# A gather, pair-product and attention-pooling tower in fp32: the last tile's bands stored by three queues and loaded by two, their wrapped columns added by TensorE, and layer 1 of rows 0 to 255 issued ahead of the tail's pooling

## What is computed

```python
row, col = np.triu_indices(33, k=1)
inner = e[:, row] * e[:, col]                        # 512 x 528 x 128
fm = relu(einsum('bpd,ad->bpa', inner, attn_W) + attn_b)
attn = softmax(einsum('ba,bpa->bp', gnn, fm), axis=1)
pooled = einsum('bp,bpd->bd', attn, inner) * 100.0
h = concatenate([gnn, pooled, gnn], axis=1)
h = maximum(h @ W_top1 + b_top1, 0)                  # 384 -> 512
h = maximum(h @ W_top2 + b_top2, 0)                  # 512 -> 256
y = h @ W_top3                                       # 256 -> 1
```

## Time and profile before

| | |
|---|---|
| Median of 3 runs | 651.45 us (651.18 to 651.52) |
| The profiled execution | 656.16 us |
| Its span, first to last instruction | 654.4 us |
| Granted TensorE clock, mean | 0.999 of full |
| TensorE matmul busy | 641.9 us (98%) |
| TensorE weight loads busy | 328.1 us (50%) |
| VectorE, ScalarE, GpSimd busy | 403.6, 417.4, 268.8 us (62%, 64%, 41%) |
| Largest group: L466, TensorE | 480.8 us |
| Its consumer: L700, ScalarE | 406.0 us |
| L531, TensorE, the pooling of `band` | 33.5 us |

### The profile page before, as it was taken

The page is one execution under the profiler, slowest core; times in us unless marked ns, Lnnn a source line. Parts: engine busy times, 40 slices in busy tenths (PEclk is TensorE's granted clock), DMA queues, the critical chain, the costliest instruction groups (busy, mean ns, idle before and its releaser), DMA issues.

```text
span 654.4 us, 22667 instructions
## 1 busy us (share of the span) xinstructions
PE 641.9 (98%) x9596; PEld 328.1 (50%) x9596; DVE 403.6 (62%) x426; ACT 417.4 (64%) x797; POOL 268.8 (41%) x208
## 2 busy tenths in 40 slices
PE   6998999999999999999999999999999999999998
PEld 2444444444444555544444555544444555544566
DVE  3564655656664677676655577766655567764763
ACT  2665666666777566676777556667677666677651
POOL 6787876685656422244746522244101011100010
PEclk9999999999999999999999999999999999999999
DMA  3211111011091111000092111000026011030010
GB/s 117 83 37 37 30 36 30 25 30 64 18 31 27 28 32 26 16 13 18 14 32 30 24 32 30 16 18 6 1 14 15 7 17 18 7 21 8 16 25 8
DMA packets 51286, 17.29 MB, mean 26 GB/s; under 512 B 47553, under 2 KB 48321, under 8 KB 51202
## 3 DMA queue, kind: packets, MB, share of 16 engines
q1 hardware_dynamic: 44738, 6.03, 11.3%
q0 software_dynamic: 4288, 8.66, 5.5%
q10 hardware_dynamic: 2176, 1.32, 0.7%
HBM read 14.10 MB, written 1.89 MB: 24 GB/s over the span
## 4 chain that ended last, share of the span: by engine, by line
PE 91%; DVE 2%; POOL 2%; DMA 2%; another core or an unknown queue 1%; issue 1%; ACT 0%; DVEq 0%; ACTq 0%
PE x_ps L466 66%; PE s_ps L478 16%; PE m_ps L531 4%; POOL rows L364 2%; DVE inner L757 2%; PE m_ps L523 1%; DMA rows<-in_table,idx 1%; PE s_ps L571 1%; PE x_ps L571 1%; PE x_ps L531 1%; DMA idx_in<-in_ids 0%; PE x_ps L560 0%; DVE e_t L809 0%; PE m_ps L560 0%
## 5 line engine op out<-in xcount | busy, mean ns | idle before, releaser
L700 ACT ACTIVATE fm<-x_ps,ab 128x352 f32<-128x352 f32 x768 | 406.0, 555 | 204.3 <-PE x_ps L466 184.2
L466 PE MATMUL x_ps<-inner,attn_w_t 128*32 128x352 f32 x6144 | 480.8, 459 | 2.2 <-issue 0.9
L466 PEld LDWEIGHTS x_ps<-inner,attn_w_t 128*32 128x32 f32 x6144 | 201.5, 110 | 229.7 <-issue 149.4
L757 DVE TENSOR_TENSOR inner<-e_t 128x2112 f32<-128x2112 f32 (+1 forms) x128 | 302.0, 2359 | 19.3 <-PE x_ps L466 16.6
L364 POOL DMA_INDIRECT rows<-in_table,idx x128 | 213.0, 1664 | 196.5 <-PE s_ps L478 179.9
L478 PE MATMUL s_ps<-fm,gnn_col 128*32 128x256 f32 (+1 forms) x2048 | 138.0, 386 | 0.0
L773 DVE COPY gnn_col<-gnn_z 128x8 f32<-128x8 f32 (+1 forms) x120 | 23.9, 199 | 180.0 <-PE s_ps L478 173.0
L478 PEld LDWEIGHTS s_ps<-fm,gnn_col 128*32 128x32 f32 x2048 | 68.7, 110 | 62.4 <-issue 20.5
L392 POOL TENSOR_TENSOR band<-band 128x192 f32<-128x192 f32 (+1 forms) x39 | 26.3, 676 | 145.6 <-DMA band<-band_scratch 145.1
L531 PE MATMUL m_ps<-band,rows 128*32 128x132 f32 x912 | 33.5, 275 | 0.0
L531 PEld LDWEIGHTS m_ps<-band,rows 128*32 128x32 f32 x912 | 27.9, 109 | 7.1
(11 more groups left out here) (57 smaller groups left out, 86.5 us busy)
## 6 DMA issues: line engine op xcount, KB each, us to landing
band<-band_scratch SPq DMA_DIRECT2D x144, 18.4 KB
rows<-in_table,idx POOLq DMA_INDIRECT x128, 2.5
band_scratch<-zeros SPq DMA_DIRECT2D x1, 784.0 KB, 3.3
w<-in_W_top ACTq DMA_DIRECT2D x3, 256.0 KB
band_scratch<-attn SPq DMA_DIRECT2D x12, 64.0 KB
gnn_z<-in_gnn_pairs SPq DMA_DIRECT2D x1, 512.0 KB
w<-in_W_top ACTq DMA_DIRECT2D x1, 512.0 KB
gnn_t<-in_gnn_cols SPq DMA_DIRECT2D x1, 256.0 KB, 3.8
```

Of the source, the lines that this page charges most:

```text
L466: mm = pe.matmul(strip(x_ps[:, (ROUNDS * slot + r) % 4, 0:ROUND], c), strip_of(attn_w_t, c), round_of(inner, slot, r), start=True, stop=True)
L700: act.activation(round_of(fm, slot, r), x_ps[:, (ROUNDS * slot + r) % 4, 0:ROUND], ACT.Relu, bias=ab[:, 0:1]).then_inc(fm_ready, 1)
L757: dve.tensor_tensor(inner[:, slot, :, :].rearrange("p q (i k) -> p q i k", k=HOPS), flat(e, at, [[P * WIDE, P], [WIDE, QUADS], [1, FIELDS] ...
```

## The change

Four things are changed together. (1) The third stage's eight stores are spread: the SP queue issues two main and one turned, the ScalarE queue two main and one turned, the GpSimd queue two turned as before. The four loads behind them go two each to the SP and the GpSimd queue. (2) GpSimd's two folds of `tail_band` are gone. TensorE adds the wrapped columns itself: `tail_group` runs the four strips with 132 columns, then the same four strips again with the wrapped columns, 4 rows of 16, accumulated on the first 16 fields of each row. (3) Layer 1 of `T01` is issued right behind layer 1 of `T2`, before any tail group; the parts are reordered to `T2, T01, T3A, T3B` on all engines, and the tail's order is written anew. (4) Layer 1 of `T3A` uses another PSUM bank (`x_ps` bank 1 in place of 3), and waits are adapted.

```diff
--- before.py
+++ after.py
@@ -80,8 +80,8 @@
 TAIL_BEFORE = 2
 MLP_CUT = LAST * P + TAIL_ROW + TAIL_BEFORE * ROWS
 
-MLP_PARTS = ((LAST * P - P, LAST * P, 0), (LAST * P, MLP_CUT, 0), (0, 2 * P, P), (MLP_CUT, BATCH, MLP_CUT - LAST * P))
-T2, T3A, T01, T3B = range(len(MLP_PARTS))
+MLP_PARTS = ((LAST * P - P, LAST * P, 0), (0, 2 * P, P), (LAST * P, MLP_CUT, 0), (MLP_CUT, BATCH, MLP_CUT - LAST * P))
+T2, T01, T3A, T3B = range(len(MLP_PARTS))
 LAG = 2
 
 
...
@@ -249,7 +250,7 @@
             n = MLP_PARTS[part][1] - MLP_PARTS[part][0]
             if part == T01:
                 return chunk(m_ps[:, c // 2, :], c % 2, 2 * P, n)
-            return chunk(x_ps[:, 3, :] if part in (T2, T3A) else m_ps[:, 1, :], c, P, n)
+            return chunk({T2: x_ps[:, 3, :], T3A: x_ps[:, 1, :], T3B: m_ps[:, 1, :]}[part], c, P, n)
 
         def layer2_psum(part, c):
             n = MLP_PARTS[part][1] - MLP_PARTS[part][0]
@@ -279,19 +280,19 @@
                                 attn[32 * q + m0:32 * q + m1, SIDE * HOPS:PAIRS],
                                 allow_slow_non_contiguous=True).then_inc(done, 16)
 
-        def issue_tail_bands(queue, stage):
-
-            if stage == 1:
-                queue.wait_ge(band_stored, bands_per_stage * (LAST + 2))
-            else:
-                queue.wait_ge(band_stored, bands_per_stage * (LAST + 3) - 16 * 2)
-                queue.wait_ge(last_turned_stored, 16 * 2)
-            first, end = ((0, EARLY_GROUPS), (EARLY_GROUPS, TAIL_GROUPS))[stage - 1]
-            for r in range(GROUP):
-                queue.dma_start(tail_band[r * SIDE:(r + 1) * SIDE, first:end, r, :],
-                                flat(band_dram, (TAIL_ROW + GROUP * first + r) * BAND,
-                                     [[WIDE, SIDE], [GROUP * BAND, end - first], [1, WIDE]])
-                                ).then_inc(tail_band_loaded[stage - 1], 16)
+        def load_tail_band(queue, stage, r, done):
+
+            first, end = ((0, EARLY_GROUPS), (EARLY_GROUPS, TAIL_GROUPS))[stage]
+            queue.dma_start(tail_band[r * SIDE:(r + 1) * SIDE, first:end, r, :],
+                            flat(band_dram, (TAIL_ROW + GROUP * first + r) * BAND,
+                                 [[WIDE, SIDE], [GROUP * BAND, end - first], [1, WIDE]])
+                            ).then_inc(done, 16)
+
+        def wait_last_bands(queue):
+
+            queue.wait_ge(band_stored, bands_per_stage * (LAST + 2) + 16 * 3)
+            queue.wait_ge(last_stored_by_act, 16 * 3)
+            queue.wait_ge(last_stored_by_pool, 16 * 2)
 
 
         tail_banks = [x_ps[:, i, :] for i in range(4)] + [m_ps[:, 0, :]]
@@ -342,10 +343,14 @@
             for k in range(L_BATCHES):
                 load_band(k % 2, POOL_N * LAST + max(k - 1, 0), ROWS * k)
             issue_bands(sp, LAST + 1, STAGE_M[1], STAGE_M[2])
-            issue_tail_bands(sp, 1)
-
-            issue_bands(sp, LAST + 2, STAGE_M[2], STAGE_M[3], turned_around=(0, 1))
-            issue_tail_bands(sp, 2)
+            sp.wait_ge(band_stored, bands_per_stage * (LAST + 2))
+            for r in range(GROUP):
+                load_tail_band(sp, 0, r, tail_band_loaded[0])
+
+            issue_bands(sp, LAST + 2, STAGE_M[2], STAGE_M[3], main=(0, 1), turned_around=(0,))
+            wait_last_bands(sp)
+            for r in (0, 1):
+                load_tail_band(sp, 1, r, tail_band_loaded[1])
             sp.wait_ge(y_ready, len(MLP_PARTS))
             sp.dma_start(out.rearrange("b o -> o b"), y[:, :]).then_inc(y_stored, 16)
             sp.wait_ge(y_stored, 16)
@@ -442,13 +447,10 @@
                 fold_next(LAST - 1, k)
             for k in range(L_BATCHES):
                 fold_batch(k % 2, pool_per_tile[k % 2] * LAST + pool_per_batch * (k // 2 + 1))
-            for stage in range(2):
-                if stage == 1:
-                    issue_bands(pool, LAST + 2, STAGE_M[2], STAGE_M[3], main=(), turned_around=(2, 3),
-                                done=last_turned_stored)
-                pool.wait_ge(tail_band_loaded[stage], 16 * GROUP)
-                lo, hi = ((0, EARLY_GROUPS), (EARLY_GROUPS, TAIL_GROUPS))[stage]
-                fold(tail_band[:, lo:hi, :, :].rearrange("p g r w -> p (g r) w"), tail_band_folded)
+            issue_bands(pool, LAST + 2, STAGE_M[2], STAGE_M[3], main=(), turned_around=(2, 3), done=last_stored_by_pool)
+            wait_last_bands(pool)
+            for r in (2, 3):
+                load_tail_band(pool, 1, r, last_loaded_by_pool)
 
 
         @block.tensor
@@ -548,6 +550,21 @@
                 pool_batch(t, GPB * k, POOL_N * t + k + 1, k % 2, POOL_N * t + k - 1 if k >= 2 else None,
                            LEFT_GROUPS if k == POOLS else GPB)
 
+            def tail_group(g):
+
+                k = g // GPB
+                fields = rows[:, LAST % BUFFERS, GPB * L_BATCHES + g, :]
+                out = tail_banks[k][:, (g % GPB) * GROUP * FIELDS:(g % GPB + 1) * GROUP * FIELDS]
+                for c in range(STRIPS):
+                    sums = strip(out, c).rearrange("p (r w) -> p r w", w=FIELDS)
+                    pe.matmul(sums, strip_of(fields, c), tail_band[:, g, :, 0:FIELDS], start=True, stop=False)
+                for c in range(STRIPS):
+                    sums = strip(out, c).rearrange("p (r w) -> p r w", w=FIELDS)
+                    mm = pe.matmul(sums[:, :, 0:HOPS], strip_of(fields, c), tail_band[:, g, :, FIELDS:WIDE],
+                                   start=False, stop=True)
+                if g % GPB == GPB - 1 or g == TAIL_GROUPS - 1:
+                    mm.then_inc(pool_done, 1)
+
             def mlp_layer1(part):
 
                 pe.wait_ge(pool_summed, pools_through(part))
@@ -566,6 +583,8 @@
                 if part == T2:
                     pe.wait_ge(w23_loaded, 32)
                     pe.wait_ge(exp_done, LAST + 3)
+                if part == T01:
+                    pe.wait_ge(pool_read, POOL_N * LAST + L_BATCHES + 1)
                 for c in chunks:
                     for k in range(C1):
                         mm = pe.matmul(layer2_psum(part, c), w2[:, k, c * P:(c + 1) * P],
@@ -653,28 +672,26 @@
             scores(STEPS * TILES - 1, 1, stop=True, reopened=True)
             mlp_layer1(T2)
 
-            for g in range(TAIL_GROUPS):
-                k = g // GPB
-                if g == 0:
-                    pe.wait_ge(tail_band_folded, 1)
-                if g == TAIL_BEFORE * GPB:
+            mlp_layer1(T01)
+
+            pe.wait_ge(tail_band_loaded[0], 16 * GROUP)
+            for g in range(EARLY_GROUPS):
+                if g == GPB * 3:
                     mlp_layer2(T2)
-                if k == 3 and g % GPB == 0:
-                    mlp_layer3(T2)
-                    mlp_layer1(T3A)
-                    mlp_layer1(T01)
-                    mlp_layer2(T3A)
-                if g == EARLY_GROUPS:
-                    mlp_layer2(T01, (0,))
-                    pe.wait_ge(tail_band_folded, 2)
-                if k == TAIL_POOLS - 1:
-                    pe.wait_ge(pool_read, POOL_N * LAST + L_BATCHES - 1)
-                pool_group(tail_banks[k], g % GPB, rows[:, LAST % BUFFERS, GPB * L_BATCHES + g, :], tail_band[:, g, :, :],
-                           g % GPB == GPB - 1 or g == TAIL_GROUPS - 1)
+                tail_group(g)
+            mlp_layer2(T01, (0,))
+            mlp_layer1(T3A)
+            mlp_layer3(T2)
+            mlp_layer2(T01, (1,))
+
+            pe.wait_ge(tail_band_loaded[1], 16 * 2)
+            pe.wait_ge(last_loaded_by_pool, 16 * 2)
+            for g in range(EARLY_GROUPS, TAIL_GROUPS):
+                tail_group(g)
+            mlp_layer2(T3A)
+            mlp_layer3(T01)
+            mlp_layer1(T3B)
             mlp_layer3(T3A)
-            mlp_layer2(T01, (1,))
-            mlp_layer1(T3B)
-            mlp_layer3(T01)
             mlp_layer2(T3B)
             mlp_layer3(T3B)
 
@@ -741,6 +758,7 @@
                     relus(base + s, s % 2,
                           stage=LAST + STAGE_M.index(s - 1) - 1 if t == LAST and s - 1 in STAGE_M else None)
             exp_rows(LAST + 2)
+            issue_bands(act, LAST + 2, STAGE_M[2], STAGE_M[3], main=(2, 3), turned_around=(1,), done=last_stored_by_act)
             for part in range(len(MLP_PARTS)):
                 mlp_relu2(part)
                 mlp_out(part)
...
@@ -952,12 +970,12 @@
             row_max(LAST + 2, STEPS * TILES)
             mlp_relu1(T2)
             normalise(LAST + 2)
+            mlp_relu1(T01)
             for k in range(TAIL_POOLS):
                 row = TAIL_ROW + k * ROWS
                 pool_sum(LAST, POOL_N * LAST + L_BATCHES + k + 1, tail_banks[k], row, min(ROWS, P - row))
-                if k == TAIL_BEFORE - 1:
+                if k == TAIL_BEFORE:
                     mlp_relu1(T3A)
-                    mlp_relu1(T01)
             mlp_relu1(T3B)
```

(7 more changed lines are left out.)

## The result

The changed kernel takes 652.94 us (median of 9 runs, 652.44 to 653.92), the kernel before, measured with it, 651.45 (9 runs). The ratio is 1.0029, with a 95% interval of 1.0021 to 1.0038: 1.9 us slower, between 1.4 and 2.5. The medians are only 1.5 apart, since the changed kernel's runs lie in two clusters, five up to 652.94 and four from 653.60 to 653.92, and the median is the top of the lower one. Forecast were 653.2 us and slower by 1.76.

A forecast was written before the change was run, and what follows sets the result against it. TensorE's work was taken to bound the kernel, in an unbroken chain behind the last scores. Passes and order, 1.61 - 0.14 + 0.18 + 0.11 = +1.76 us on 651.45, gave 653.2 us, range 651.9 to 654.9.

The forecast's parts named there:

- What bounds the kernel: Tail behind the last scores: the chain runs through TensorE unbroken from 631.83 to 647.88, with no DMA or fold in it.
- The wrapped pass: Tail groups on TensorE: each added pass of 64 columns costs 0.115 us, 14 of them +1.61 us (1.48 to 3.19).
- The rival that priced a pass by what it issues: Tail groups: a wrapped pass costs 0.228 us, like one of 132 columns; +3.3 us, 654.8 us; chance 0.20.
- The order: TensorE's tail: one run of groups fewer -0.14, other work before the last four groups +0.18, end of tail +0.11 us.
- The gap that VectorE leaves there: Between layer 1 and layer 2 of `T3B`, ending at 3.58 and starting at 4.29 after the last group: 0.71 us.
- The sum: Whole tail: 1.61 - 0.14 + 0.18 + 0.11 = +1.76 us.
- The margin of the transfers: Ahead of group 10: late bands ready 1.3 us early before, loads landed some 4 us early after; faster transfers gain 0 us.
- The rival that ended faster: Ahead of group 10: before's timed runs wait for late bands, 3.2 us at 4.5 us lateness; 650.0 us; faster, chance 0.09.
- The unscaled sum: Whole kernel: the 4.7 us between profiled execution and median lies outside the tail, so +1.76 us is added unscaled.
- the second rival: Wait ahead of group 10: late bands were waited for in timed runs, which the change ends; 650.0 us; faster, chance 0.09.

The follow-up runs named there:

- 16-column kernel: The changed kernel with wrapped columns of only one row in four, so a pass's matmuls have 16 columns, not 64; 652.75 us, one run.
- the kernel with folds kept: The changed kernel with both folds back on GpSimd and no wrapped columns on TensorE; spread and new order stay; 651.42 us, ratio 1.0001 to before.
- the spread alone: The kernel before with only the third stage's stores on three queues and its loads on two; 650.90 us, ratio 0.9993 to before.

## Why the prediction was right

**What bounds the kernel.** Right, and shown from two sides: removing only the passes takes the time back to before, and making only the transfers faster leaves the tail at 20.95 us.

**The wrapped pass.** Forecast 0.115 us from the line through 132 and 352 columns, 14 of them 1.61. The chain shows 0.11 and 0.12, and the two pairs of kernels that differ by the passes show 1.64 and 1.55. The rival that priced a pass by what it issues, at 0.228, is refuted. The Trainium skill's floor of about 25 ns between the starts of two matmuls (page "TensorE: Matmul & The Clock Gate", section "Wait — 56ns, not 53.3ns?") would have made a pass 0.20 us, an estimate from that page, if it held for matmuls in different strips. The chain's 0.115 for eight records says it does not. I had written that before's trace neither confirms nor refutes the rule, from a mean of 28 ns a record. Read one by one, the same records already refute it between strips: in a group of before the matmuls of the four strips start at 633.219, 633.225, 633.232 and 633.239, and the next in the first strip 115 ns after its predecessor. The 16-column kernel, with 26 ns and more between starts in the same strip, doesn't contradict the rule within a strip.

**The order.** The term had the right sign and was too small, 0.15 in all; the traces show 0.35 to 0.45. Two errors are in it, and they partly cancel. Up to the end of the last group the forecast was 0.18 - 0.14 = +0.04; the kernel with folds kept has it at 640.39 - 626.75 = 13.64 us, before at 13.80, so it is -0.16. The missing gain is layer 1 of `T3A`, taken as unchanged: 1.06 us in before, 0.86 now. From the last group to the end of the last layer 2 the term was +0.11; it is 648.02 - 641.40 = 6.62 us, in the forecast 6.21, before 6.10, so +0.52. Layer 2 of `T3A` took 1.96, not 1.76, layer 1 of `T3B` 1.02, not 0.80, the last layer 2 1.99, not 1.92, and layer 3 of `T01` 0.95, not 1.02. The old values are steps between starts in before's chain, where a neighbour covers part of the operation: layer 1 of `T3B` is 0.80 as a step and 0.97 by its own row. A step's share in a chain isn't its price in another place. The gap that VectorE leaves there, 0.70 us, was forecast (0.71).

**The sum.** 1.76 forecast, 1.99 in the tail of the trace, 1.9 in the timed runs (1.4 to 2.5). The pass is the large term and was right for its reason. That the rest came within 0.2 us is in part luck, since the two errors of the order have opposite signs.

**The margin of the transfers.** Right in both orders, though smaller than forecast after the change: the late loads landed 639.89 - 636.60 = 3.3 us before TensorE took them, and some 4 were expected. The rival that ended faster, with bands awaited in the timed runs, finds no support: the spread alone shows at most 1.0 us of gain at the interval's end, and the tail doesn't move. That the timed runs had a small wait which no profile shows can't be excluded by this: it would have to be below that.

**The unscaled sum** stood on the difference of 4.7 us between the profiled execution and the median lying outside the tail. That was right: the profile of the spread alone has the same tail of 20.95 us with last scores 4.6 us sooner. But the difference isn't one between a profiled and a timed execution. It is one between chips, 655.82 against 651.30 us for before, so it says nothing about how late transfers land in timed runs, for which I had used it against the second rival.

## What to carry to other kernels

In this kernel the chain ran through one engine without a gap, and there moving work from an idle engine onto it was paid in full, though it shortened a transfer's path; first find out by how much the path is early. The same two edits (late groups' wrapped passes, spread queues) were worth 0.6 and 0.35 us by the traces once other savings on TensorE had left it waiting for the bands. And a small matmul that is hardly shorter than a larger one is worth merging with it: layer 2 took 1.92 us for 32 rows and 1.98 for 128, with weight loads in work for 1.86 us of either.

Compare stretches from a common event, here the last scores, and not spans: the spans of before (654.4 us) and of the spread alone (649.8) differ by 4.6 us with the same tail.

## What the runs showed of the hardware

Four strips of 32 stationary columns side by side, fp32, each matmul two records: one record in each of the four strips takes 114 ns with 132 moving columns, 57 to 61 ns with 64 and 26 to 32 ns with 16, from start to start in one strip. The records of neighbouring strips start at most 12 ns apart. With 64, 132 and 352 columns the price lies on one line (0.115, 0.228 and 0.592 us a pass) that leaves 0.01 us at zero columns, so the loads and matmuls issued add nothing else that shows; only the 16-column pass shows a floor.
